# VectorE computes a hidden unit's low part before it adds a down result

## The reference, cut to what matters

```
x = x + layernorm(attention(layernorm(x)))
y = layernorm(x)
gate_e = y @ Wg[e];  up_e = y @ Wu[e]          # 256 x 256 each, e = 0..7
h_e    = silu(gate_e) * up_e
ffn    = sum over e of route[:, e] * (h_e @ Wd[e])
out    = x + layernorm(ffn)
```

## Time and profile before

| | |
|---|---|
| median of 3 runs | 1497.04 us (1494.59 to 1497.18) |
| profiled execution | 1496.2 us, span in the trace 1494.5 us |
| granted PE clock, mean | 0.995 |
| PE busy | 98% of the span |
| DVE busy | 69% |
| ACT busy | 43% |
| POOL busy | 30% |
| DMA | 16 GB/s over the span |

### The profile page before, as it was taken

How to read it: one execution, slowest core, us unless ns; L and a number is a source line. 1 busy time by engine, 2 the same in 40 slices (tenths; PEclk the granted TensorE clock), 3 DMA queues, 4 the chain that set the end, 5 groups by cost and what they waited for, 6 DMA issues and landing times. The chain is left out here.

```text
span 1494.5 us, 37390 instructions
## 1 busy us (share of the span) xinstructions
PE 1465.5 (98%) x14438; PEld 1279.1 (86%) x14438; DVE 1023.8 (69%) x2492; ACT 647.2 (43%) x1189; POOL 442.9 (30%) x653
## 2 busy tenths in 40 slices
PE   7799999999999999999999999999999999999997
PEld 6688888888888888888888888888888888888886
DVE  6667667676776767667675776767667676776765
ACT  5443534445354443534445354443534445344333
POOL 1403414133251233414134141232413234141231
PEclk9899999999999999999999999999999999999999
DMA  5100000000000000000000000000000000000000
GB/s 171 57 2 15 15 0 14 14 14 14 0 18 10 14 14 9 19 0 14 14 14 14 0 14 14 14 14 0 28 0 14 14 14 14 0 14 16 2 8 22
DMA packets 25345, 24.59 MB, mean 16 GB/s; under 512 B 2016, under 2 KB 25056, under 8 KB 25312
## 3 DMA queue, kind: packets, MB, share of 16 engines
q1 hardware_dynamic: 25312, 24.13, 5.1%
HBM read 15.74 MB, written 8.39 MB: 16 GB/s over the span
## 5 line engine op out<-in xcount | busy, mean ns | idle before, releaser
L1002 DVE TENSOR_TENSOR late<-late,up_ps 128x512 f32<-128x512 f32 x256 | 174.9, 683 | 155.7 <-PE up_ps L436 99.1
L705 ACT ACTIVATE h_hi<-late 128x512 fp32r<-128x512 f32 x256 | 161.6, 631 | 247.2 <-DVE late L1002 247.2
L436 PE MATMUL down_ps<-w_hi,h_hi 128*128 128x256 f32 x976 | 264.5, 293 | 0.0
L786 ACT ACTIVATE late<-gate_ps 128x512 f32<-128x512 f32 x256 | 152.3, 595 | 252.1 <-PE gate_ps L436 252.1
L436 PE MATMUL down_ps<-w_hi,h_lo 128*128 128x256 f32 x976 | 254.1, 282 | 0.0
L1225 POOL TENSOR_TENSOR rms_in<-rms_in,minus_half 128x16 f32<-128x16 f32 x32 | 93.4, 2919 | 498.3 <-DVE rms_in L958 498.3
L899 DVE TENSOR_TENSOR h_lo<-late,h_hi 128x512 fp32r<-128x512 f32 x256 | 175.7, 686 | 65.0 <-ACT h_hi L705 65.0
L1024 DVE SCALAR_TENSOR_TENSOR late<-down_ps,route,late 128x256 f32<-128x256 f32 x364 | 158.4, 477 | 87.9 <-PE down_ps L436 84.9
L436 PE MATMUL gate_ps<-ft_hi,w_hi 128*128 128x512 f32 x512 | 204.9, 400 | 1.0 <-ACT ft_hi L705 0.8
L436 PE MATMUL gate_ps<-ft_hi,w_lo 128*128 128x512 f32 x512 | 203.5, 397 | 0.0
L436 PE MATMUL up_ps<-ft_hi,w_hi 128*128 128x512 f32 x512 | 199.7, 390 | 0.0
(11 more groups left out here) (170 smaller groups left out, 2481.9 us busy)
## 6 DMA issues: line engine op xcount, KB each, us to landing
xs<-in_x SPq DMA_DIRECT2D x32, 256.0 KB, 2.9
out_rows<-late SPq DMA_DIRECT2D x32, 256.0 KB, 2.2
late<-in_wg SPq DMA_DIRECT2D x7, 256.0 KB, 4.1
late<-in_wu SPq DMA_DIRECT2D x7, 256.0 KB, 4.4
late<-in_wd SPq DMA_DIRECT2D x6, 256.0 KB, 4.2
late<-in_wkv_t SPq DMA_DIRECT2D x1, 512.0 KB, 3.9
x<-in_wd SPq DMA_DIRECT2D x2, 256.0 KB, 4.6
late<-in_wq_t SPq DMA_DIRECT2D x1, 256.0 KB, 4.6
```

The lines of the kernel that those rows point to most:

```text
L436: last = nc.tensor.matmul(dst, lhs, rhs, start=n == 0, stop=n == len(terms + low_terms) - 1)
L705: return nc.scalar.activation(dst, src, ACT.Copy)
L786: nc.scalar.activation(h_f[:, m, :], gate_ps[:, :], ACT.Silu).then_inc(silu_ready[0], 1)
L1002: nc.vector.tensor_tensor(h_f[:, m, :], h_f[:, m, :], up_ps[m][:, :], ALU.mult).then_inc(h_ready[0], 1)
```

## The change

In `rest`, on DVE alone, `low_hidden(e, m, f)` comes before `add_down(e - 1, m, f)`, in all twelve slots of each pass. No instruction is added or taken away, and the queues of the other engines stay as they are. `first_expert`, the units of expert 0 and the last block are not touched; in the latter two the low part stands ahead of the addition already.

```
@@ -1104,8 +1104,8 @@
                     for m in range(MT):
                         hidden(e, m, f)
                         attention(4 * e - 4 + 2 * m, a)
+                        low_hidden(e, m, f)
                         add_down(e - 1, m, f)
-                        low_hidden(e, m, f)
                         attention(4 * e - 3 + 2 * m, a)
```

## The result

The changed kernel takes 1507.11 us in the median of 6 runs (1505.65 to 1509.0), the kernel before 1496.41 us in 6 runs beside it. The ratio is 1.0076 with a 95% interval of 1.0065 to 1.0087: 10.7 us slower, where 10.8 us were forecast. The profiled execution took 1508.33 us with a span of 1506.6 us.

The account below looks back on a forecast made before the run. PE, busy for 98% of the span, was taken as the bound. Per pass 1.02 + 0 - 0.30 = 0.72 us, by 15 passes 10.8 us, on 1496.2 us gave 1507.0, with 0.84 for the median 1507.8 us; range 1502.5 to 1515.

Parts of the forecast that it names:

- Step 1: Slot (4, 0): addition queued behind the low part, which waits for ACT's high part, delays down(3, 1); 1.02 us lost a pass.
- The restart: PE's second matmul starts 0.28 or 0.34 us after DVE's instruction ends, from two trace places; slot (4, 0)'s loss 0.99 to 1.05.
- Step 2: Slot (3, 0): addition over at 738.73 instead of 738.13, just ahead of down(2, 1); loss 0 to 0.1 us, taken as 0.
- the prediction's own last sign: The forecast is wrong if PE shows no wait in slot (4, 1), or if it waits in a second slot.
- Step 3: Slots (6, 0) to (7, 1): low part fills a gap, the chain to the "ft" transposes starts earlier; gain 0.30 us a pass.
- The upper bound of 0.42 us: Most that the "ft" transposes could begin earlier per pass, without their wait.
- The nine other slots: They cost nothing; least slack from addition to down is 0.7 us, in slot (6, 1), and 1.1 us and more elsewhere.
- The sum: Per pass 1.02 + 0 - 0.30 = 0.72 us, by 15 passes 10.8 us.
- (b): Not slower: down(3, 1) isn't held, needing ACT's high part by about 748.9, not 749.91; 1492.5 us; faster 0.04, same 0.05.
- (c): More downs caught: slot (3, 0) costs 0.1 us, low-slack slots some 0.3 us, no gain; 1518 us, chance 0.08.
- (d): The granted clock falls in PE's gap, 2.8 us lost a pass; 1550 us, chance 0.03.

Follow-up runs that it names:

- e1_only_40: The kernel before, with the low part ahead of the addition in slot (4, 0) alone, all 15 passes: 1511.37 us, ratio 1.0099.
- e9_low_behind_pool: The kernel before with slot (6, 0) alone exchanged, and slot (7, 0)'s low part held until POOL's scale and shift are written: 1490.25 us.
- the copy in the old order: The kernel before plus one useless ACT copy of 128x512 in front of the high part in slot (4, 0): 1499.26 us, ratio 1.0019.
- e3_high_early: The changed kernel, with ACT's high part in slot (4, 0) ahead of the attention step's copies and squares: 1492.60 us, ratio 0.9978.
- e2_all_but_40: The changed kernel, but with slot (4, 0) in the old order: 1492.85 us, ratio 0.9974 to the kernel before.
- e7_new_copy: The changed kernel plus one useless ACT copy of 128x512 in front of the high part in slot (4, 0): 1516.58 us, ratio 1.0136.

## Why the prediction was right

**Step 1, slot (4, 0).** Forecast 1.02 us a pass, measured 0.97 (all of it in slot (4, 1), as said) and 0.99 by the pass of e1_only_40. The mechanism stands on three runs of different kinds: that slot alone brings the whole loss, an early high part takes it away, and a high part that is 0.52 us later makes it 0.52 us larger. The restart was as in the earlier trace rows: from the addition's end at 757.43 to the second matmul at 757.71 it is 0.28 us, so the lower of the two rows was the right one, and the taken mean was 0.03 us too much. The other 0.02 us PE made up within the twelve matmuls behind the wait.

**Step 2, slot (3, 0).** Taken as 0 with a bound of 0.1 us, measured 0.06. The addition's start was put at 0.60 us behind the low part's, and there it is 0.72. This also touches the prediction's own last sign, that it is wrong if PE waits in a second slot: strictly, that sign came true, in the last pass alone, with 0.18 us; in the others the 0.06 us doesn't show as a wait. It is too small to change the account.

**Step 3, slots (6, 0) to (7, 1).** Forecast 0.30 us a pass, measured 0.28. It is the exchange in slot (6, 0) alone that makes it. The count of 15 was too high: the first pass had no wait at "ft", as the 13 waits of the earlier trace rows leave open, and the last gained 0.20 us. The upper bound of 0.42 us was too high as well: in e9_low_behind_pool, with nothing lost at "ft", the pass is 0.38 us shorter.

**The nine other slots.** Forecast nothing, and PE's lag doesn't change in any of them. From the addition's end to the down that needs it the changed kernel has 0.76 us in slot (6, 1), as said, but 0.92 us in slot (7, 0), where at least 1.1 was claimed. The working didn't list every consumer either: the slack of norm_apply in slot (4, 1), less than 0.1 us, was missed, and it took the copy in the old order to find it. For this change it was covered by the argument that DVE is 0.46 us late there and PE 1.02; by these numbers it would have cost with PE on time, which no run shows by itself.

**The sum.** 0.97 + 0.06 - 0.28 = 0.75 us against 0.72; three errors of 0.02 to 0.06 us that partly cancel. That the medians differ by 10.7 us where 10.8 were forecast is closer than the working deserves: by PE's lag in the profiled executions the fifteen passes cost 11.7 us, and the interval of the times reaches from 9.7 to 13.0 us. The mechanism was right; the agreement to 0.1 us is luck.

**The rivals.** (b), not slower, is what e3_high_early makes of the same order. The condition was the one that was named, though the high part is about 5 us earlier there and not 1, so the 1 us itself wasn't tried. (c), more downs caught by PE's new rhythm, is refuted by the changed kernel's own trace, in which PE's lag grows in slots (3, 1) and (4, 1) alone; e2_all_but_40, which has no such delay of PE, can't speak to it. (d), the clock: the granted clock of the loop is 1.00 in both kernels from 170 to 1341.6 us, and the mean of the profiled execution 0.994 against 0.995. Gaps of 1 us in 91 don't lower it here.

**The rule of the banks.** The Trainium skill, page Perfetto Trace Analysis, section Optimizing Tensor Performance, wants matmul groups to rotate through PSUM banks. The trace bears it out in slot (4, 0) with 0.97 us, in slot (3, 0) with 0.06, and in none of the ten others. With a single bank the kernel is exposed, but as long as the addition ends before the next down, behind the twelve up matmuls, the exposure costs nothing.

## What to carry to other kernels

Before two instructions of an in-order queue change places, ask for each which engine waits for it and how soon: here the low part was needed an expert later and the addition by the very next product of the bound engine. A gap on an engine that isn't the bound is no reason to fill it. Where it is filled, decide place by place: eleven of these twelve exchanges gained 3.8 us together, all of it in slot (6, 0), and the twelfth lost 14.8.

## What the runs showed of the hardware that wasn't expected

A multiply of 128x2 elements on POOL took 0.20 us by itself and 0.66 to 0.67 us when DVE's low part, a subtraction of two SBUF operands, had started 0.07 to 0.08 us before it; it ended 0.05 us after DVE did. Holding DVE back restored the 0.20 us. The changed kernel has a second case in the same step of part 0: with the low part of slot (6, 1) now started 0.16 us ahead of it, POOL's first multiply takes 0.55 us instead of 0.20, and ends 0.05 us after DVE. The Trainium skill, page SBUF — State Buffer, section Who interferes with whom, has a rule for it: a DVE instruction with two SBUF inputs and a GpSimd instruction that reads SBUF share a read interface, and the one that issues second is held until the first is done. The traces here agree.

PE went on without extra cost after a gap of 0.7 or 1.2 us: in the changed kernel and in e7_new_copy the second matmul after the wait is where the restart rows put it, and the matmuls behind it keep their distance of 0.11 to 0.12 us.
